# Normalised tokens by scalar_tensor_tensor instead of tensor_scalar, in a local transformer and three attentions

## What is computed

```
def _layernorm(x, axis=-1, eps=1e-05):
    m = jnp.mean(x, axis=axis, keepdims=True)
    v = jnp.var(x, axis=axis, keepdims=True)
    return (x - m) / jnp.sqrt(v + eps)

x = x + tanh(g_xattn[0]) * L0_xattn(_layernorm(x), ctx, ctx)          # 16 heads, causal
x = x + tanh(g_ffn[0])   * L0_ffn(_layernorm(x))                      # 6 layers, local attention + GEGLU
x = x + tanh(g_xattn[1]) * L1_xattn(_layernorm(x), ctx)
x = x + tanh(g_ffn[1])   * L1_ffn(_layernorm(x))                      # 8 experts
x = x + tanh(g_xattn[2]) * L2_xattn(_layernorm(x), ctx, ctx, side)    # 16 heads
x = x + tanh(g_ffn[2])   * L2_ffn(_layernorm(x))                      # 1 shared + 8 experts
x = x + tanh(g_xattn[3]) * L3_xattn(_layernorm(x), ctx)               # linear attention
x = x + tanh(g_ffn[3])   * L3_ffn(_layernorm(x))

# in each of the 6 layers of L0_ffn, on tokens of which half the columns come from the token before:
mu = x.mean(-1, keepdims=True); var = ((x - mu) ** 2).mean(-1, keepdims=True)
xn = (x - mu) / jnp.sqrt(var + 1e-05) * g + bln
hg = xn @ W1 + b1; a, gate = jnp.split(hg, 2, -1)
return a * jax.nn.gelu(gate, approximate=False) @ W2 + b2
```

## Time and profile before

| | us |
|---|---|
| median of 3 runs | 3037.59 |
| the three runs | 3037.59, 3028.44, 3041.67 |
| the profiled execution's own time | 3020.22 |
| its span, first to last instruction | 3018.3 |

### The profile page before, as it was taken

One profiled execution on the slowest core, in us unless ns is written; L12 is line 12 of the kernel. 1 busy time (PEld: TensorE's weight loads), 2 busy tenths in 40 slices (PEclk: granted clock), 3 DMA queues, 4 the chain that ended last, 5 costly groups with the idle time before them and its releaser, 6 DMA issues.

```text
span 3018.3 us, 102967 instructions
## 1 busy us (share of the span) xinstructions
PE 2655.5 (88%) x41282; PEld 1957.5 (65%) x41282; DVE 2088.2 (69%) x4954; ACT 1729.9 (57%) x3705; POOL 1297.8 (43%) x1689
## 2 busy tenths in 40 slices
PE   7789999999899999999899999998897877998875
PEld 5556666666566666666666666666676866998655
DVE  6777777777777777777777777776466667554662
ACT  5466666666666666666666666666342255222442
POOL 5555445445445445445445544544231055000660
PEclk9899999999999999999999999999797999999997
DMA  2100001000100001000100000000002000000004
GB/s 77 62 15 11 14 14 50 14 14 11 52 15 11 14 15 49 14 14 11 53 14 11 14 16 15 11 14 15 4 4 75 0 5 5 1 0 0 5 3 140
DMA packets 50942, 66.57 MB, mean 22 GB/s; under 512 B 24506, under 2 KB 30085, under 8 KB 49285
## 3 DMA queue, kind: packets, MB, share of 16 engines
q1 hardware_dynamic: 50820, 64.87, 7.7%
HBM read 38.23 MB, written 1.05 MB: 13 GB/s over the span
## 4 chain that ended last, share of the span: by engine, by line
PE 67%; DVE 17%; issue 5%; ACT 4%; POOL 3%; SPq 1%; DVEq 1%; DMA 1%; POOLq 0%; ACTq 0%
PE ps L720 12%; PE ps L798 6%; PE ps L784 5%; PE ps L759 5%; PE ps L817 5%; PE ps L901 3%; PE ps L824 3%; PE ps L768 3%; PE ps L889 3%; PE ps L888 3%; DVE xn L1847 2%; PE ps L791 2%; DVE area L1825 2%; ACT xnT L1061 2%; PE ps L751 2%
## 5 line engine op out<-in xcount | busy, mean ns | idle before, releaser
L1061 ACT ACTIVATE area<-ps 64x128 f32<-64x128 f32 (+5 forms) x1532 | 772.7, 532 | 486.8 <-PE ps L726 123.6
L1443 POOL TENSOR_TENSOR area<-area 128x512 f32<-128x512 f32 x384 | 488.7, 1273 | 890.4 <-DVE area L1795 890.4
L1449 POOL TENSOR_TENSOR area<-area,rnq 128x512 f32<-128x512 f32 x384 | 396.5, 1043 | 14.4 <-ACT rnq L1188 0.6
L720 PE MATMUL ps<-lw,area 128*128 128x512 f32 x768 | 397.9, 621 | 0.7 <-ACT area L1061 0.7
L1779 DVE TENSOR_REDUCE ssq<-area 128x8 f32<-128x512 f32 x384 | 261.4, 681 | 36.6 <-ACT area L1170 23.8
L1857 DVE SCALAR_TENSOR_TENSOR area<-ps,lcol,area 128x128 f32<-128x128 f32 (+1 forms) x288 | 83.0, 344 | 269.2 <-ACT area L1211 265.0
L1795 DVE TENSOR_TENSOR area<-ps,table 128x512 f32<-128x512 f32 x384 | 261.4, 681 | 0.0
L1793 DVE TENSOR_TENSOR area<-ps,table 128x512 f32<-128x512 f32 x384 | 257.2, 670 | 0.0
L1170 ACT ACTIVATE area<-ps 128x512 f32<-128x512 f32 x384 | 227.3, 592 | 43.0 <-PE ps L720 42.7
L726 PE MATMUL ps<-ident,area 128*128 128x128 f32 x1536 | 232.5, 274 | 7.5 <-POOL area L1449 7.5
L1261 ACT ACTIVATE area<-ps 128x256 f32<-128x256 f32 x208 | 80.0, 385 | 242.8 <-PE ps L889 242.8
(11 more groups left out here) (278 smaller groups left out, 5716.2 us busy)
## 6 DMA issues: line engine op xcount, KB each, us to landing
lvm<-area SPq DMA_DIRECT2D x384, 65.0 KB
lw<-in_wqkv SPq DMA_DIRECT2D x6, 1536.0 KB
area<-in_moe_w SPq DMA_DIRECT2D x32, 256.0 KB, 3.0
lw<-in_wout SPq DMA_DIRECT2D x6, 512.0 KB
ctxT<-in_ctxT SPq DMA_DIRECT2D x64, 38.5 KB, 1.8
lw<-in_wff SPq DMA_DIRECT2D x6, 341.0 KB
lw<-in_moe_g SPq DMA_DIRECT2D x1, 1152.0 KB
lw<-in_moe_u SPq DMA_DIRECT2D x1, 1152.0 KB
```

The source lines that it names most:

```text
L720: nc.tensor.matmul(ps[s][:, j, :], xsT[s], wqkv[w.p][:, j * 512:(j + 1) * 512], start=True, stop=True).then_inc(l_qk_ps, 1)
L1061: return nc.scalar.activation(dst, src, ACT.Identity if kw else ACT.Copy, **kw)
L1443: pool.tensor_tensor(QR[s][:, cols], QR[s][:, cols], RA[s][:, cols], ALU.add).then_inc(l_rsum, 1)
L1449: pool.tensor_tensor(rows, rows, rnq[s][:, 8 * j:8 * j + 8, None].to_broadcast([S, 8, LD]), ALU.mult).then_inc(l_qkn, 1)
```

## The change

In three places the instruction that writes the normalised tokens changes from tensor_scalar, (source - mean) * rs with mean and rs both read as one value per partition, to scalar_tensor_tensor. There the mean is still one value per partition, and `rs`, a 128x1 tile, is the second tensor operand, repeated over the columns with a step of 0. What is computed, the waits, the semaphores and the position of every instruction on every engine are the same: on DVE these instructions differ in their opcode, and on the other engines nothing differs. The normalisations at lines 1601, 1635 (the second attention), 1849 and 1583 are not touched.

```diff
@@ -1713,8 +1713,8 @@
                 def normalised(s, it):
                     dve.wait_ge(ln_rstd, nth(no, it, s))
-                    V.tensor_scalar(xn[s][:, :], X[:, it * G + s, :], mv[s][:, 0:1], rs[s][:, 0:1],
-                                    ALU.subtract, ALU.mult).then_inc(x_normed, 1)
+                    V.scalar_tensor_tensor(xn[s][:, :], X[:, it * G + s, :], mv[s][:, 0:1], rs[s][:, 0:1].to_broadcast([S, D]),
+                                           ALU.subtract, ALU.mult).then_inc(x_normed, 1)
@@ -1844,8 +1844,8 @@
             def shifted_normed(s, w):
                 dve.wait_ge(l_rs, nth(0, w.it, s))
-                V.tensor_scalar(xn[s][:, 0:64], y1[s][:, 0:64], mv[s][:, 0:1], rs[s][:, 0:1],
-                                ALU.subtract, ALU.mult).then_inc(l_xn, 1)
+                V.scalar_tensor_tensor(xn[s][:, 0:64], y1[s][:, 0:64], mv[s][:, 0:1], rs[s][:, 0:1].to_broadcast([S, 64]),
+                                       ALU.subtract, ALU.mult).then_inc(l_xn, 1)
                 V.tensor_scalar(xn[s][:, 64:128], ps[s][:, 3, 0:64], mv[s][:, 0:1], rs[s][:, 0:1],
                                 ALU.subtract, ALU.mult).then_inc(l_xn, 1)
```

## The result

The changed kernel is slower: 3046.55 us in the median of 20 runs against 3031.74 us in the median of 20 runs of the kernel before, ratio 1.0039 with a 95% interval of 1.0025 to 1.0054. The forecast was 3036 and no measurable difference. The 20 runs are not one cluster: 5 lie between 3030 and 3035 us, 15 between 3043 and 3055, and none between. The profiled execution took 3046.18 us, so it belongs to the upper group. The 20 runs of the kernel before lie between 3026.86 and 3041.67 us without such a gap, and its profiled execution, at 3020.22, is faster than all of them: the two profiled executions lie 26 us apart, the medians 14.8.

A forecast was written before the change was run, and what follows sets the result against it. The prediction took PE to wait on DVE's lines 1847 and 2013, held off by POOL. With that wait kept, the tail's -2 us, line 1716 at 0, gave a median of 3036 us; range 2984 to 3052.

The forecast's parts named there:

- What bounds the kernel: DVE's lines 1847 and 2013 wait some 0.57 and 0.77 us for POOL, on the chain; worth at most 66 us.
- Does the new form wait?: Lines 1847 and 2013 go on waiting for POOL's lines 1449 and 1495 in the new form; chance 0.72.
- the one row of line 1508: Linear attention: POOL's line 1508 lost 0.37 us to DVE's two-tensor line 2078; exclusion assumed in the other direction too.
- rival A: New form doesn't wait for POOL: line 1847 saves 43 us, line 2013 11 us, giving 2984 us; chance 0.18.
- B: Line 2013 alone, in the linear attention, gets to the port before POOL: 11 us saved, 3026 us; chance 0.05.
- C: Line 1847 is also passed over by POOL's next instruction, line 1443: 114 us lost, 3152 us; chance 0.05.
- The tail behind POOL's end: With the wait kept, time after POOL's end at lines 1847 and 2013 changes: -24 to +4 us, taken as -2.
- The price without a wait: New form unhindered: 352 ns for 128 columns against line 1716's 338, 294 ns for 64; line 1716's effect put at 0.
- The sum: Profiled execution 3020.2 - 2 = 3018 us; the same -2 on the median of the runs gives 3036 us.
- The spread of the runs: Runs differ by 13 us among themselves; this widened the range for the forecast's own case to 3008 to 3052 us.

## Why the prediction was wrong

**What bounds the kernel.** Right. The waits inside lines 1847 and 2013 were read rightly as POOL's, and they stood on the chain.

**Does the new form wait?** Right, and taken from the one row of line 1508: the exclusion holds in the other direction too. Rivals A, B and C fall with the medians of 919 and 1178 ns; C would have shown 2.1 us.

**The tail behind POOL's end.** The term was mis-sized. Between -8 and +4 us I took -2, since the new form might start as soon as POOL has read its last column. It does not: line 1847 has 30 ns more and line 2013 66, within 5 ns of the high end (35 and 69). By rows that is 96 x 0.030 + 15 x 0.066 = 3.9 us instead of -2. The price without a wait was 10 ns too high: 342 ns for line 1716 where 352 were expected, 284 for the one line 1847 that doesn't wait where I had 294.

**The sum.** Here is the step that failed. "+35 ns for line 1847 and +69 for line 2013 [...] all on the chain" priced a longer wait of PE by its length. It had no term for the granted clock. In the linear attention the wait costs more than its length, since it stands where PE is idle already: 0.86 us and then 0.46. With 0.07 more, in the profiled execution, the projection behind the wait runs at 1.2 GHz and a sequence costs 1.6 us more, 12 of them some 19 us. Of the 14.8 us between the medians the rows give the longer waits 3.9; the other 11 are put down to the clock, an estimate by difference. The windows before showed a clock of 1.00 in that stage from 2820 us on, and I didn't look at what holds it there. The experiments show it from both sides: the delay alone brings the loss (1.0037), busy matmuls in the wait take it away (0.9992), and with the wait itself gone the new form costs nothing that can be measured (0.9959 against 0.9961 with the old).

**The spread of the runs.** The forecast used the 13 us between the runs of the kernel before as scatter. Some of it has a cause. With the wait of the old form the clock can fall too: of the four profiled executions that have it, two got into the long distance and two (the kernel before, and the one in which POOL waits in the local transformer) didn't. There it can end within the stage; with 0.06 to 0.07 us more all three profiled executions got into it, and it ended in none. That the two groups of runs, at 3030 to 3035 and 3043 to 3055 us, are executions without and with it is an inference from the profiled ones and from the granted clock of each of the 20 runs: 0.965 to 0.968 in the lower group, 0.958 to 0.964 in the upper. It isn't the whole of the scatter: ahead of the linear attention, leaving out that same kernel with the wait in the local transformer, the profiled executions already differ by 15 us (first start of line 2013: between 2780.1 and 2795.6 where line 1847 has the old form, between 2789.4 and 2795.5 with the new).

**What stays open.** Why an execution gets into the long distance at the fourth sequence in one case and not in another. Why it lasts longer with the longer wait: the slow stretch left line 933 by about 0.10 us a sequence at distances of 10.1 and by about 0.03 at 10.2, and both executions that ended had it far from where it began, which fits, but no run varied it by itself. And whether rival A's 43 us in the local transformer exist: no kernel was tried in which line 1847 doesn't wait and POOL isn't held back either.

## What to carry to other kernels

Changing tensor_scalar into an instruction that reads two SBUF tensors doesn't take it out of POOL's way: look at what POOL runs beside it, and see whether POOL has slack to give way (the linear attention had, 0.9961; the local transformer had not, 1.0024). Before adding even 70 ns to a wait of PE, look at how idle PE is around that place and whether the granted clock stands at 1.00 there; if it does, the price of falling is that of the matmuls behind the wait at half speed. Where repeated runs fall in two groups, compare the distance between repetitions in each stage, in more than one profiled execution, before calling it scatter.

## What the runs showed of the hardware

- A vector instruction with two SBUF tensors that starts 0.2 us behind the start of a POOL tensor_tensor of 128x512 waits until that has ended: 919 ns for 64 columns, where 284 ns are enough without. It ends 30 ns later than a tensor_scalar in the same place, for 64 columns, and 66 ns for 128. The Trainium skill (VectorE: DVE Perf Modes, section "Mode 2×_2P — use both read ports for one tensor") says that a float32 tensor_scalar within SBUF gives two results a cycle and a tensor_tensor one. With the 0.96 GHz that the page counts with that is, as an estimate, a difference of 0.52 ns a column; 30 ns over 64 columns and 66 over 128 are 0.47 and 0.52, so the rows agree.
- Two idle times of PE in a repetition of 8.6 us, neither of them over 0.94 us, can let the granted clock fall to its lower level for the matmuls behind them, in every repetition, at 1.6 us each. With 0.86 and 0.46 us it fell in two of four profiled executions and came back within the stage; with 0.06 to 0.07 us more it fell in three of three and stayed for the dozen repetitions that were left.
- A memset of one column behind a vector instruction delays a semaphore by nothing (1.17 us with and without); one of 64 columns by 0.06 to 0.07 us.
